# Attention and experts in one pipeline: score units issued in pairs, weighted values of eight heads in one PSUM slot

## What is computed

```python
def _stablemax3_s(x):
    pos = 1.0 + x * (1.0 + 0.5 * x * (1.0 + x / 3.0))
    neg = 1.0 / (1.0 - x * (1.0 - 0.5 * x * (1.0 - x / 3.0)))
    return jnp.where(x >= 0, pos, neg)
# logits minus their row maximum, then s / sum(s)

x = x + attention(layernorm(x))          # q k^T * hd**-0.5 -> stablemax3 -> @ v -> @ w_out.T + b_out
x = x + experts(layernorm(x))            # router softmax, top 2 of 4, gates renormalised
# h = silu(xf @ w1[e]) * (xf @ w3[e]);  out = sum_e gates[:, e] * (h @ w2[e])
```

## Time and profile before

| | us |
|---|---|
| median of 3 runs (1258.78 to 1259.63) | 1258.8 |
| profiled execution, its own time | 1257.9 |
| its span, first to last instruction | 1256.2 |
| TensorE busy | 1180.1 |
| VectorE busy | 1034.1 |
| ScalarE busy | 1027.1 |
| POOL busy | 328.0 |

### The profile page before, as it was taken

The page is one execution under the profiler, slowest core; times in us unless marked ns, Lnnn a source line. Parts: engine busy times, 40 slices in busy tenths (PEclk is TensorE's granted clock), DMA queues, the critical chain, the costliest instruction groups (busy, mean ns, idle before and its releaser), DMA issues.

```text
span 1256.2 us, 29583 instructions
## 1 busy us (share of the span) xinstructions
PE 1180.1 (94%) x10244; PEld 952.3 (76%) x10244; DVE 1034.1 (82%) x2030; ACT 1027.1 (82%) x1102; POOL 328.0 (26%) x706
## 2 busy tenths in 40 slices
PE   2569999999999999999999999999999999999988
PEld 1337777888777788877778877778887777888778
DVE  4876888988888898888888888889888888988833
ACT  2587888888888888889988888898888888888872
POOL 4212333221233222223322222332212233231111
PEclk9988999999999999999999999999999999999999
DMA  5111211121210112211111211111122111111000
GB/s 169 60 61 61 64 34 43 56 64 64 64 61 28 47 54 64 64 64 55 35 43 58 64 64 64 49 41 39 63 64 64 64 43 34 51 64 61 11 5 9
DMA packets 83617, 67.90 MB, mean 54 GB/s; under 512 B 6656, under 2 KB 82048, under 8 KB 83584
## 3 DMA queue, kind: packets, MB, share of 16 engines
q1 hardware_dynamic: 83584, 67.47, 16.9%
HBM read 45.42 MB, written 20.97 MB: 53 GB/s over the span
## 4 chain that ended last, share of the span: by engine, by line
PE 81%; DVE 7%; issue 4%; DMA 4%; ACT 3%; SPq 1%; POOL 0%; DVEq 0%; POOLq 0%; ACTq 0%
PE up_a L757 15%; PE up_b L757 14%; PE up_a L915 10%; PE up_b L915 10%; PE sc L818 9%; PE pv L773 6%; PE sc L898 6%; DMA q_stack<-m_split 3%; PE pv L837 2%; PE misc L850 2%; DVE mx L667 1%; PE misc L873 1%; PE pv L873 1%; DVE xn_T L675 1%; PE misc L955 1%
## 5 line engine op out<-in xcount | busy, mean ns | idle before, releaser
L447 ACT ACTIVATE w_sq<-sc 128x1024 f32<-128x1024 f32 x256 | 262.7, 1027 | 126.8 <-PE sc L818 125.7
L576 DVE SCALAR_TENSOR_TENSOR poly<-w_sq,sc 128x1024 f32<-128x1024 f32 x256 | 310.7, 1214 | 21.0 <-ACT w_sq L447 20.6
L667 DVE TENSOR_REDUCE mx<-sc 128x4 f32<-128x1024 f32 x256 | 304.5, 1213 | 9.8 <-PE sc L898 9.8
L568 DVE TENSOR_TENSOR hid<-silu_a,up_b 128x512 f32<-128x512 f32 x256 | 176.0, 687 | 105.5 <-PE up_b L757 45.8
L488 ACT ACTIVATE poly<-poly,two 128x2048 f32<-128x2048 f32 x128 | 252.1, 1993 | 0.4
L493 ACT ACTIVATE poly<-poly 128x2048 f32<-128x2048 f32 x128 | 243.2, 1901 | 0.0
L470 ACT ACTIVATE silu_a<-up_a 128x512 f32<-128x512 f32 x256 | 153.4, 599 | 56.9 <-PE up_a L757 51.9
L757 PE MATMUL up_a<-xn_hi,w_hi 128*128 128x256 f32 x512 | 167.3, 327 | 1.4 <-ACT silu_a L470 1.4
L366 POOL TENSOR_TENSOR x_resb<-x_res,b_out_all 128x128 f32<-128x128 f32 x64 | 27.8, 456 | 492.9 <-DVE y_acc L638 471.3
L757 PE MATMUL up_b<-xn_hi,w_hi 128*128 128x256 f32 x512 | 154.0, 301 | 0.7 <-DVE y_acc L683 0.5
L773 PE MATMUL pv<-poly,v_pad 128*32 128x256 f32 x2048 | 140.9, 394 | 7.0 <-ACT poly L493 6.6
(11 more groups left out here) (102 smaller groups left out, 1833.5 us busy)
## 6 DMA issues: line engine op xcount, KB each, us to landing
qk_scratch<-qk_split SPq DMA_DIRECT2D x32, 512.0 KB, 2.8
q_stack<-qk_scratch SPq DMA_DIRECT2D x128, 128.0 KB, 2.7
k_stack<-qk_scratch SPq DMA_DIRECT2D x128, 128.0 KB, 2.8
x_in<-in_L_attn_x_dram SPq DMA_DIRECT2D x32, 128.0 KB, 2.1
x_res<-in_L_attn_x_dram SPq DMA_DIRECT2D x32, 128.0 KB, 2.4
out_dram<-y_acc SPq DMA_DIRECT2D x32, 128.0 KB, 1.8
poly<-in_L_ffn_w_dram SPq DMA_DIRECT2D x2, 1024.0 KB, 9.2
q_stack<-m_split SPq DMA_DIRECT2D x64, 16.0 KB
```

Source lines behind the costliest of these rows:

```text
L447: nc.scalar.activation(w_sq[:, u % 2, :], sc[:, u % 2, :], ACT.Square).then_inc(sq_ok, 1)
L568: nc.vector.tensor_tensor(hid[:, 2 * u:2 * u + 2, :].rearrange("p a t -> p (a t)"), silu_a[:, u % 2, :], up_b[:], ALU.mult).then_inc(hid_o ...
L576: nc.vector.scalar_tensor_tensor(poly[:, u, :], w_sq[:, u % 2, :], 3.0, sc[:, u % 2, :], ALU.add, ALU.mult).then_inc(poly_ok, 1)
L667: nc.vector.tensor_reduce(by_row[:, :, 2 * g:2 * g + 2], sc[:, u % 2, :].rearrange("p (j k t) -> p j k t", j=2, k=2), AX.X, ALU.min, negat ...
```

## The change

Two things are changed together.

*Units in pairs.* TensorE issues distance units 0 and 1, 2 and 3, 4 and 5, 6 and 7 directly one behind the other, and the scores too; between the pairs stand two expert units or, in the second half, the expert outputs. `down(2)` is cut into its two token halves. ScalarE and VectorE get new orders to go with it: hid(u) stands behind poly(u) for u from 2 on, hid(7) behind the residual, and in the second half statistics, expert sums and router steps shift by a unit.

*Eight heads in one slot.* `v_pad` has 48 columns per head, values from column 16. For an even group the window starts at column 16, for an odd one at column 0, so that the values of head j of the odd group fall on rows 16 to 24 of the same 32 partitions, and both groups are summed into one slot of `pv`. The four groups fill `pv` once. One copy on ScalarE, four transposes into `misc`, one reciprocal of 32 columns and two multiplies replace two copies, eight transposes, two reciprocals and two multiplies.

```diff
-        v_pad = [sb(f"v_pad{i}", [128, C, H, 32]) for i in range(2)]
+        v_pad = [sb(f"v_pad{i}", [128, C, H, 48]) for i in range(2)]
...
+                silu(0)
+                square(0)
+                square(1)
+                if has(i, off - 1):
+                    act.wait_ge(pv_full, G * n)
+                    after(act, oq_full, n - 1)
+                    nc.scalar.copy(o_T[:], pv[:]).then_inc(o_ok, 1)
+                silu(1)
+                square(2)
+                silu(2)
...
+                square(3)
+                silu(3)
+                square(4)
+                silu(4)
...
+                def normalized():
+                    m = n - 1
+                    by_head = misc[:].rearrange("p (a j b e) -> p a j b e", a=C * G // 2, j=4, e=16)
+                    dve.wait_ge(oq_full, m + 1)
+                    nc.vector.reciprocal(den_r[:], misc[:].rearrange("p (h e) -> p h e", e=16)[:, :, HD]).then_inc(den_ok, 1)
...
                 for u in range(U):
-                    if has(i, off - 2):
+                    if u < 2 and has(i, off - 2):
                         hidden(u)
                     if has(i, off):
                         polynomial(u)
+                    if u >= 2 and has(i, off - 2) and u < U - 1:
+                        hidden(u)
...
-                    if u == 7 and has(i, off):
-                        dve.wait_ge(pv_full, G * n + 2)
-                        after(dve, oq_full, C * n)
-                        nc.vector.tensor_copy(o_T[:, 0:2, :], pv[:]).then_inc(o_ok0, 1)
...
+                first = 16 - 16 * (g % 2)
                 for c in range(C):
                     for j in range(4):
                         at = (2 * (j % 2) + j // 2) * S
-                        last = nc.tensor.matmul(pv[32 * j:32 * j + 32, g % 2, :], v_pad[par][:, c, 4 * g + j, :],
-                                                poly[:, C * g + c, at:at + S], start=(c == 0),
-                                                stop=(c == C - 1))
+                        last = nc.tensor.matmul(pv[32 * j:32 * j + 32, g // 2, :],
+                                                v_pad[par][:, c, 4 * g + j, first:first + 32],
+                                                poly[:, C * g + c, at:at + S], start=(g % 2 == 0 and c == 0),
+                                                stop=(g % 2 == 1 and c == C - 1))
...
+                two_distances(0)
+                if has(i, off - 1):
+                    weighted_values(i, off - 1, 3)
+                ups(1)
...
+                two_distances(2)
+                ups(2)
...
+                ups(3)
+                two_distances(4)
+                ups(4)
...
+                ups(5)
+                two_distances(6)
+                ups(6)
...
+                ups(7)
...
+                two_scores(0)
+                if has(i, off - 2):
+                    down(0, (0, 1))
+                two_scores(2)
+                if has(i, off - 2):
+                    down(1, (0, 1))
+                    down(2, (0,))
+                two_scores(4)
+                if has(i, off - 2):
+                    down(2, (1,))
+                if has(i, off):
+                    weighted_values(i, off, 0)
+                two_scores(6)
+                if has(i, off - 1):
+                    router_operand()
+                if has(i, off - 2):
+                    down(3, (0, 1))
+                if has(i, off - 1):
+                    router_logits()
```

More of the change, by code:

```diff
@@ L443, in square @@
                 def square(u):
+                    if not has(i, off):
+                        return
                     k = U * n + u
@@ new lines, in first_half @@
+                silu(1)
+                square(2)
+                silu(2)
+                if has(i, off + 1):
+                    m, par = n + 1, (off + 1) % 2
+                    act.wait_ge(v_full, m + 1)
+                    act.wait_ge(consts_v, 4)
+                    after(act, pv_full, G * (m - 1))
+                    for c in range(C):
+                        last = nc.scalar.copy(v_pad[par][:, c, :, 16:16 + HD],
+                                              pv[:, 0, c * D:(c + 1) * D].rearrange("p (h d) -> p h d", d=HD))
+                    last.then_inc(v_ok, 1)
@@ new lines, in first_half @@
+                square(3)
+                silu(3)
+                square(4)
+                silu(4)
+                square(5)
+                silu(5)
+                if has(i, off - 1):
+                    m = n - 1
+                    act.wait_ge(attnT_full, m + 1)
+                    after(act, res_full, m)
+                    nc.scalar.copy(attn_T[:], misc[:, 0:S]).then_inc(attnT_ok, 1)
+                square(6)
+                silu(6)
+                square(7)
+                silu(7)
@@ L510, in second_half @@
                         log_of(g + 1)
[L511 to L516, removed]
                     if g == G - 1 and has(i, off - 1):
@@ L523, in second_half @@
                         weights_of(g)
+                    if g == 1 and has(i, off - 1):
+                        m = n - 1
+                        act.wait_ge(xn2T_full, m + 1)
+                        after(act, xn2_lo_ok, m)
+                        after(act, lg_full, m)
+                        nc.scalar.copy(xn2_T[:], misc[:, 0:S]).then_inc(xn2_out, 1)
             act.wait_ge(consts_v, 4)
@@ L612, in first_half @@
                         polynomial(u)
+                    if u >= 2 and has(i, off - 2) and u < U - 1:
+                        hidden(u)
                     if u in (1, 2, 3, 4) and has(i, off - 2):
                         gate_step(u - 1)
[L615 to L626, removed]
+                    if u == 3 and has(i, off - 1):
+                        normalized()
                     if u == 4 and has(i, off + 2):
@@ new lines, in first_half @@
+                ups(1)
+                if has(i, off + 1):
+                    m = n + 1
+                    after(pe, o_ok, n)
+                    for c in range(C):
+                        last = nc.tensor.matmul(pv[:, 0, c * D:(c + 1) * D], xn_T[:, c * 128:(c + 1) * 128],
+                                                proj_T[:, 2, :], start=True, stop=True)
+                    last.then_inc(v_full, 1)
+                two_distances(2)
+                ups(2)
+                if has(i, off - 1):
+                    m = n - 1
+                    pe.wait_ge(o_ok, m + 1)
+                    if has(i, off + 1):
+                        pe.wait_ge(qk_out, n + 2)
+                    else:
+                        pe.wait_ge(lg_ok, m)
+                        if has(i, off):
+                            pe.wait_ge(m_ok, n + 1)
+                    for c in range(C):
+                        for a in range(G // 2):
+                            at = (c * G // 2 + a) * 128
+                            last = nc.tensor.transpose(misc[:, at:at + 128], o_T[:, a, c * 128:(c + 1) * 128], ident[:])
+                    last.then_inc(oq_full, 1)
@@ L912, in down @@
                         pe.wait_ge(acc_ok, E * C * m + C * (e - 1))
-                    for c in range(C):
+                    for c in chunks:
                         for f in range(FB):
@@ L917, in down, with two_scores @@
                                                     w2_sb[:, FB * e + f, :], start=(f == 0), stop=(f == FB - 1))
-                    last.then_inc(down_full, 1)
+                    if chunks[-1] == C - 1:
+                        last.then_inc(down_full, 1)
+                def two_scores(u):
+                    if has(i, off + 1):
+                        scores(u)
+                        scores(u + 1)
                 def maxima_T():
```

133 lines of the change are left out of this document (52 added, 81 removed).

## The result

| | before | after |
|---|---|---|
| median, us | 1259.2 (4 runs) | 1279.4 (4 runs) |
| span of the profiled execution | 1256.2 | 1278.8 |
| TensorE / VectorE / ScalarE busy | 1180.1 / 1034.1 / 1027.1 | 1145.3 / 1011.7 / 1025.4 |

The account below looks back on a forecast made before the run. TensorE, busy 94%, bounds the kernel; 2.05 us less work against waits of 4.20 instead of 0.7 was taken as +1.05 us in each of 29 periods: 1257.9 + 30.5 + 0.9 = 1289 us. Range 1260 to 1308.

Parts of the forecast that it names:

- D3: Distance unit 3, first half, on TensorE: waits 1.63 us for poly(1), behind hid(1) and SiLU(1), to free its sc half.
- D5: Distance unit 5, first half, on TensorE: waits 0.38 us for poly(3) to free its half of sc.
- D7: Distance unit 7, first half, on TensorE: waits 0.54 us for poly(5) to free its half of sc.
- S3: Scores unit 3, second half, on TensorE: waits 0.59 us for the second maximum on VectorE.
- the rival of a small loss: Waits grow only 2.3 to 2.7 us because VectorE catches up: +0.25 to +0.65 a period, 1266 to 1278; chance 0.10.
- Work saved: TensorE's own work per period falls 2.05 us: merged units 0.76, passages 0.28, transposes 0.53, second half 0.48.
- The timetable walked through: Chain walked on TensorE, ScalarE and VectorE from D0 to the next D0: period 38.03 us, +1.24.
- two end points: Period change: +0.87 us with hand-overs at 0.05 instead of 0.12, +1.24 as walked through; +1.05 taken between them.
- my end of +1.45: Upper end point for the period: 0.2 us more for normalisation on strided rows of misc, +1.45 us.
- The covers hold: Waits grow by less than 2.05 us, decided at D3, so the change wins; 1199 if none grows; faster case 0.09.
- The clock falls: Pauses bring TensorE to 1.2 GHz in one period of ten: 2 us more a period on average, 1348; chance 0.04.
- TensorE busy near 34: Sign in the profile after: TensorE busy near 34 us of a period of 37.7 to 38.1 us.

Follow-up runs that it names:

- experiments 1 and 6: Poly(1) ahead of hid(1) on VectorE: 1 on the changed kernel, 1238.3 us; 6 on the changed kernel with weighted values as before the change, 1254.1 us.
- experiment 5: Changed kernel with SiLU(1) ahead of the copy of o_T on ScalarE: 1273.8 us.
- number 10: Changed kernel with poly(1) ahead of hid(1), v_pad's copies ahead of SiLU(2), x_in's statistics behind unit 5 instead of 4, scores in pairs: 1228.2 us.
- experiment 7: Changed kernel with distances issued one at a time in the order before the change, scores still in pairs, packing kept: 1280.6 us.
- number 8: Changed kernel with poly(1) ahead of hid(1), v_pad's copies ahead of SiLU(2), x_in's statistics behind unit 5, scores one at a time: 1230.0 us.

## Why the prediction was right, and where it was off

**Sign and mechanism** were right: the pairs expose a chain over ScalarE and VectorE, with its largest wait at D3, and the smaller ones at D5 and D7, S3 and L964 in the places named. Forecast and measured waits: D3 1.63 and 1.44, D5 0.38 and 0.44, D7 0.54 and 0.45, up_b for hid(4) 0.06 and 0.26, S1 0.13 and 0.09, S3 0.59 and 0.60, S7 0.08 and 0.03, L964 0.40 and 0.41, D0 0.39 and 0.28. VectorE's busy time was forecast at 31.0 a period and is 31.02. Of the chain to D3, experiments 1 and 6 show the order of hid(1) and poly(1) and experiment 5 the copy; that SiLU(1) stands behind two squares was not tried in another order. The waits at D5 and D7 are shown by place, and by number 10 together: it shortens both chains and gains 10 us on the first experiment.

**The size** was off: +30.5 us were forecast and +20.1 measured, +1.05 a period against +0.73. The period of 37.53 lies below the 37.7 to 38.1 that I named as a sign. The total of 1279.4 lies near the low end of the forecast, 1.4 us above the rival of a small loss, whose reason (VectorE catching up at S3 and D7) is not what happened: S3 waits as forecast. Two terms were mis-sized:

- *Work saved.* All waits, the nine above and 0.05 at S5, sum to 4.05 against the 4.20 of the forecast. From D0 to D0 the period is 37.44 (594.96 to 632.40), 33.39 without them; before it is 36.71 (585.52 to 622.23), 35.96 without its 0.54 in front of L927 and 0.21 in front of D0, read by starts. So TensorE lost some 2.6 us of work where I counted 2.05: 1.87 instead of 1.57 in the first half, 0.70 instead of 0.48 in the second. This is the larger part of the miss: the timetable's period of 38.03 is 0.59 too long, and 38.03 - 4.20 = 33.83 of work in it against 33.39 makes 0.44 of that, the waits 0.15. One item is the *transposes*: I put 0.53 for the four on o_T that go, read where a unit of distances followed, and the four that stay cost 0.36 (602.36 to 602.72) now that ups follow them, so 0.70 went.
- *The wait of D3*, 0.19 less than forecast. Some 0.09 of it are the hand-overs, for which I used 0.12 throughout: VectorE to TensorE takes 0.05 (poly(1) done at 600.34, D3 at 600.39), ScalarE to VectorE 0.10 (598.42 to 598.52). Another 0.08 comes from D2, which starts later than I had it, because the projection of the values holds TensorE for 0.54 (598.17 to 598.71) and not for 0.46. The 0.14 that I read in front of L927 is not an error: the same 0.14 stands in front of L964, between the end of the logits at 626.72 + 0.23 = 626.95 and 627.09. The hand-over differs from place to place, and at D3, D5, D7 and S3 it is 0.05 to 0.06, near my low end.

```profile
626.72 0.23 DVE L712 TENSOR_TENSOR logits<-misc,router_b_all 128x4 f32<-128x4 f32 x2 [0.32 <-PE misc L989]
```

The timetable walked through came to +1.24; that I took +1.05 instead was a choice between two end points, and it happened to go the right way.

**Packing** I had priced at four transposes and 0.9 us of VectorE: 0.53 on TensorE is 15 us; alone it gave 11.6. **Scores in pairs** were forecast neutral to slightly bad (18.96 against 18.78) and are neutral. **The normalisation** costs 0.34 for the reciprocal of 32 columns and 0.49 for two multiplies, against 0.25 and 0.29 twice: at the middle of my bounds, and my end of +1.45 for it was not needed. **Fill and drain** were put at zero. The 22.6 us by which the span grew less 21.2 leave 1.4 for them, from one profiled execution of each kernel; executions of the changed kernel differ by 2.7 us, so this isn't told from zero.

**Rivals.** *The covers hold*: no, but its hinge was the right one: cutting it at D3 turns the loss into a gain of 20 us. *The clock falls*: not in the changed kernel's loop, where it is 1.00 throughout. Its mean is 0.988 against 0.991 before, and the low stretches are in the filling and the draining. The rival is not empty, though: in experiment 7 it fell to 0.50 three times in the loop, each time at the end of a pause of 1.48 us, at a price of 1.5 us each, which is far from the 59 us that I had put. *TensorE busy near 34*, which I named as a mark, came out at 35.03, because overlapping records hide part of the short waits (D5's 0.44 by starts stands in the record as 0.18): starts tell more than busy time here.

## What to carry to other kernels

When work is issued in pairs on one engine, walk the queues of the engines that must empty the buffers between two pairs, and put there first what frees the second buffer; work of another stream (here the experts' product, which was needed only when its bank was due again) belongs behind it. The exchange has a price, since that work now comes later: in number 8, where two more links are moved as well, up_b waits 0.65 us a period for hid instead of 0.26. The saving of a merge (0.19 us) is small against one wrongly placed link (1.4 us), and both together can still win: the same change with two instructions exchanged is 1.6% faster than the kernel before instead of 1.6% slower. A wait that goes at one place should be looked for at the next instruction that needs the same queue or the same buffer (L857 in experiment 5, S1 in experiment 7).

## What the runs showed of the hardware

The same four transposes hold TensorE for 0.53 us when 62-row units follow (rows 3) and for 0.36 when 128-row matmuls of the experts follow. From the end of the releasing instruction on VectorE to the start of the waiting matmul it takes 0.05 us at D3 and 0.14 us at L964. A merged unit costs 0.24 us in the loop of every kernel here that has one unheld, as rows 3 had it. With one pause of some 1.5 us a period directly behind a unit (experiment 7) the granted clock stayed at 1.00 in most periods and fell to 0.50 in three, and 16 matmuls of the experts' output then took 3.29 us instead of 2.05.
